# Cross-attention and mixture-of-experts in two layers: the second layer's keys made between the pieces of the first layer's shared expert

## The reference

```
x = x + tanh(g_xattn[0]) * cross_attention_0(layernorm(x), ctx)
x = x + tanh(g_ffn[0])   * (shared_expert(n) + routed_experts(n, top 1 of 8))   # n = layernorm(x)
x = x + tanh(g_xattn[1]) * cross_attention_1(layernorm(x), ctx)
x = x + tanh(g_ffn[1])   * mixture_1(layernorm(x), top 2 of 8)

def _swiglu(x, wg, wu, wd):
    return jax.nn.silu(x @ wg.T) * (x @ wu.T) @ wd.T
shared_out = _swiglu(x, shared_gate, shared_up, shared_down)      # layer 0, hidden width 512
k = (y @ Wk + bk).reshape(B, M, NUM_HEADS, HEAD_DIM)              # layer 1: y is ctx, not x
```

## Time and profile before

| | us |
|---|---|
| median of 3 runs | 1487.17 (1486.02 to 1487.17) |
| the profiled execution | 1488.32 |
| its span | 1486.5 |
| TensorE busy | 1352.8 (91% of the span) |
| ScalarE busy | 982.6 (66%) |
| VectorE busy | 539.6 (36%) |
| GpSimd busy | 175.0 (12%) |

### The profile page before, as it was taken

The page is one execution under the profiler, slowest core; times in us unless marked ns, Lnnn a source line. Parts: engine busy times, 40 slices in busy tenths (PEclk is TensorE's granted clock), DMA queues, the critical chain, the costliest instruction groups (busy, mean ns, idle before and its releaser), DMA issues. The chain is left out here.

```text
span 1486.5 us, 31922 instructions
## 1 busy us (share of the span) xinstructions
PE 1352.8 (91%) x13236; PEld 715.3 (48%) x13236; DVE 539.6 (36%) x1204; ACT 982.6 (66%) x1178; POOL 175.0 (12%) x188
## 2 busy tenths in 40 slices
PE   7799999999999996999869999999999985399994
PEld 4433333333333653899733334334334323299983
DVE  7412142241433253333461123322422433644435
ACT  4499999999997233222259995995995980155532
POOL 2000000000000330233300000000000000166530
PEclk9899999999999998999978999999999997599997
DMA  7671010101001814111338010110111215012223
GB/s 208 157 125 27 20 27 20 27 20 27 23 20 28 294 57 151 58 50 47 104 110 149 20 28 14 34 27 16 34 27 47 65 33 167 18 62 75 72 67 157
DMA packets 65867, 100.82 MB, mean 68 GB/s; under 512 B 10075, under 2 KB 47967, under 8 KB 64953
## 3 DMA queue, kind: packets, MB, share of 16 engines
q1 hardware_dynamic: 59768, 82.47, 20.5%
q0 software_dynamic: 5952, 16.26, 3.4%
HBM read 67.99 MB, written 26.21 MB: 63 GB/s over the span
## 5 line engine op out<-in xcount | busy, mean ns | idle before, releaser
L1232 ACT ACTIVATE arena<-ps 128x1024 f32<-128x1024 f32 x556 | 554.5, 1224 | 56.7 <-PE ps L998 56.7
L998 PE MATMUL ps<-arena 99*32 99x512 bf16 x6656 | 465.5, 384 | 16.8 <-PEq L848 10.9
L998 PEld LDWEIGHTS ps<-arena 99*32 99x32 bf16 x6656 | 149.8, 95 | 408.5 <-issue 168.2
L1232 ACT ACTIVATE wqkv<-ps 128x1024 f32<-128x1024 f32 x276 | 294.9, 1225 | 22.7 <-PE ps L998 22.7
L1014 PE MATMUL ps<-arena 128*32 128x512 f32 x2224 | 289.7, 593 | 1.3 <-ACT arena L1232 0.8
L1314 DVE COPY work<-ps 128x512 f32<-128x512 f32 x32 | 22.1, 691 | 406.6 <-PE ps L1014 406.6
L1704 PEld LDWEIGHTS ps<-work,arena 128*128 128x128 f32 x1184 | 145.1, 196 | 6.4 <-DVE work L1801 3.4
L1704 PE MATMUL ps<-work,arena 128*128 128x128 f32 x1184 | 146.2, 279 | 2.1 <-DVE work L1801 2.1
L1014 PE MATMUL ps<-wqkv,arena 128*32 128x512 f32 x1104 | 143.9, 593 | 0.0
L1905 POOL DMA_INDIRECT work<-xn_img,fetch x62 | 60.3, 973 | 613.4 <-POOLq L978 596.8
L1716 PE MATMUL ps<-arena,work 128*128 x496 | 117.2, 380 | 0.0
(11 more groups left out here) (206 smaller groups left out, 1158.7 us busy)
## 6 DMA issues: line engine op xcount, KB each, us to landing
arena<-in_ew SPq DMA_DIRECT2D x16, 512.0 KB, 5.6
arena<-q_img SPq DMA_DIRECT2D x32, 192.0 KB
arena<-y_tok SPq DMA_DIRECT2D x12, 512.0 KB, 6.3
arena<-k_img SPq DMA_DIRECT2D x8, 624.0 KB, 13.3
q_img<-work SPq DMA_DIRECT2D x18, 256.0 KB, 2.5
k_img<-work SPq DMA_DIRECT2D x21, 208.0 KB, 2.5
arena<-q_img SPq DMA_DIRECT2D x32, 128.0 KB
work<-work SPq DMA_DIRECT2D x128, 32.0 KB, 1.9
```

What stands on the lines that cost most here:

```text
L998: last = nc.tensor.matmul(ps[i * VW:(i + 1) * VW, buf + j, :], k2[0:ROWS + SHIFT, h, at:at + VW], q2[0:ROWS + SHIFT, h, :], start=True, st ...
L1232: nc.scalar.activation(probs[(b * STEPS + u) % RING], ps[:, buf:buf + 2, :], ACT.Exp, scale=SCALE).then_inc(s_exp, 1)
```

## The change

The core of the diff:

```diff
-                    def k_item(n):
-
-                        for ko in range(KD):
-                            if n:
-                                pe.wait_ge(s_kh, (n - 1) * KD + ko + 1)
-                            project_k(1, ko, n, (7, 5)[ko]).then_inc(s_kp, 1)
+                    def k_half(n, ko):
+                        if n == 0 and ko == 0:
+                            pe.wait_ge(s_tok, 1)
+                            pe.wait_ge(s_wk[1], 48)
+                        elif ko == 0:
+                            pe.wait_ge(s_kh, n * KD)
+                        else:
+                            pe.wait_ge(s_kh, n * KD + 1)
+                        project_k(1, ko, n, 5).then_inc(s_kp, 1)
...
                         shared_up(3, 0)
+                        k_half(0, 0)
                         shared_down(2)
-                        for f in range(1, 4):
-                            shared_up(3, f)
+                        k_half(0, 1)
                         lists()
+                        k_half(1, 0)
+                        shared_up(3, 1)
+                        k_half(1, 1)
+                        k_norm(0)
...
                         shared_down(3)
-                        pe.wait_ge(s_sy, NT)
-                        pe.wait_ge(s_wk[1], 48)
-                        k_item(0)
-                        for n in range(1, 4):
-                            k_item(n)
-                            k_norm(n - 1)
                         k_norm(3)
...
+                    def k_half(n, ko):
+                        act.wait_ge(s_kp, n * KD + ko + 1)
+                        if ko == 0:
+                            if n:
+                                act.wait_ge(s_kl, n)
+                            if n >= 2:
                                 act.wait_ge(s_kd[n % 2], 48)
+                        src = ps[:, 5, 0:KB]
+                        nc.scalar.activation(full1[:, ko, :], src, ACT.Copy)
...
+                        places()
+                        split_keys(0)
+                        shared_hidden(3, 0)
+                        shared_hidden(3, 1)
+                        for n in range(1, 3):
+                            split_keys(n)
+                            shared_hidden(3, n + 1)
+                        split_keys(3)
+                        for t in range(TB):
+                            n = TB * GP + t
+                            dve.wait_ge(s_sd, n + 1)
...
+                        for n in range(4):
+                            sp.wait_ge(s_kl, n + 1)
+                            store_parts(sp, k_img[1], part1[n % 2], slice(n * KB, (n + 1) * KB), False, s_kd[n % 2])
+                        sp.wait_ge(s_e, 16 * (2 * E + DOWN_KEPT))
                         sp.wait_ge(s_sd, NT)
                         sp.wait_ge(s_sx, TB * GP)
                         for e in range(DOWN_KEPT, E):
                             load_down(sp, e)
...
+                        sp.wait_ge(s_kd[0], 96)
...
-                        sp.wait_ge(s_e, 16 * 3 * E)
...
                     def down(i):
+                        if l == 0 and i == 0:
+                            pe.wait_ge(s_e, 16 * 3 * E)
```

More of the change, by code:

```diff
@@ L250, in build @@
         w_now[1][1], at = view(work, at, [KD, F])
-        at = 2 * KD * QB
+        _, at = view(work, 2 * 2 * NT * E, [layers[0].slots, 3 * (layers[0].tiles + 1)], BF16)
+        _, at = view(work, at, [layers[0].slots, P], BF16)
+        full1, at = view(work, at, [KD, KB])
         part1 = [[None] * 3, [None] * 3]
@@ L256, in build @@
                 part1[i][j], at = view(work, at, [KD, KB], BF16)
[L257 to L260, removed]
         TS = 2 * NT
@@ L947, in layer @@
                                                   for w in ("up", "act", "hidden", "down", "out", "added"))
-            s_kp, s_kf, s_kh, s_ks, s_kn = (only(l == 0, f"k1_{w}")
-                                            for w in ("projected", "full", "high", "squared", "summed"))
+            s_kp, s_kh, s_ks, s_kn = (only(l == 0, f"k1_{w}")
+                                            for w in ("projected", "high", "squared", "summed"))
+            s_pl = only(l == 0, "places_made")
             s_kr, s_km, s_kl = (only(l == 0, f"k1_{w}") for w in ("rest", "mid", "low"))
@@ L1262, in shared_out @@
                                                  scale=tgate[:, 2:3]).then_inc(s_sy, 1)
[L1264 to L1269, removed]
-                                act.wait_ge(s_kd[n % 2], 48)
[L1271 to L1276, removed]
+                    def k_half(n, ko):
[4 more added lines that the diff above has]
+                            if n >= 2:
+                                act.wait_ge(s_kd[n % 2], 48)
+                        src = ps[:, 5, 0:KB]
+                        nc.scalar.activation(full1[:, ko, :], src, ACT.Copy)
+                        if n >= 2 and ko == 0:
+                            act.wait_ge(s_kn, n - 1)
+                        nc.scalar.activation(squares1[n % 2][:, ko, :], src, ACT.Square).then_inc(s_ks, 1)
+                        nc.scalar.activation(part1[n % 2][0][:, ko, :], src, ACT.Copy).then_inc(s_kh, 1)
                     if l == 1:
@@ L1296, in _ @@
                             shared_act(2, f)
+                        shared_act(3, 0)
+                        k_half(0, 0)
                         shared_out(2)
[L1298 to L1301, removed]
+                        k_half(0, 1)
+                        k_half(1, 0)
+                        shared_act(3, 1)
+                        k_half(1, 1)
+                        k_half(2, 0)
+                        shared_act(3, 2)
+                        k_half(2, 1)
+                        k_half(3, 0)
+                        shared_act(3, 3)
+                        k_half(3, 1)
                 @block.vector
@@ L1495, in places @@
                                                              in1=pad[:, 0:NTL], op0=ALU.add, op1=ALU.add))
-                        nc.vector.tensor_scalar(fetch[:, 0:NTL], dest[:, 0:NTL], S - 1, None, ALU.bitwise_and)
+                        last = nc.vector.tensor_scalar(fetch[:, 0:NTL], dest[:, 0:NTL], S - 1, None, ALU.bitwise_and)
+                        if l == 0:
+                            last.then_inc(s_pl, 1)
                     def shared_hidden(b, f):
@@ L1509, in _ @@
                     else:
[L1510 to L1518, removed]
@@ L1519, in _, with split_keys @@
-                        places()
-                        for n in range(4):
+                        def split_keys(n):
                             dve.wait_ge(s_kh, KD * (n + 1))
-                            nc.vector.tensor_tensor(rest1, full1[n % 2], part1[n % 2][0], ALU.subtract
-                                                    ).then_inc(s_kr, 1)
+                            nc.vector.tensor_tensor(full1, full1, part1[n % 2][0], ALU.subtract).then_inc(s_kr, 1)
                             dve.wait_ge(s_kr, n + 1)
-                            nc.vector.tensor_copy(part1[n % 2][1], rest1).then_inc(s_km, 1)
+                            nc.vector.tensor_copy(part1[n % 2][1], full1).then_inc(s_km, 1)
```

22 lines of the change are left out of this document (16 added, 6 removed).

## The result

The changed kernel takes 1483.66 us (median of 12 runs, 1481.10 to 1486.93), the kernel before 1486.51 in the same comparison (12 runs, 1484.90 to 1491.21): a ratio of 0.9982 with an interval of 0.9974 to 0.9991. The forecast was 1482.7, with a range of 1480.4 to 1486.7.

A forecast was written before the change was run, and what follows sets the result against it. SyncE's last issue was taken to bound the routed experts' start: 2.2 us from TensorE's earlier norm plus 2.3 from SyncE's shorter tail give 4.5, from median 1487.17 to 1482.7 us; range 1480.4 to 1486.7.

The forecast's parts named there:

- a landing of the first fetch over 6 us: Sign of being wrong: GpSimd's first fetch for the routed experts takes over 6 us from issue, against 4.9 forecast.
- The wait for `s_tok`: Before the first key half, TensorE would idle 1.96 us until VectorE's L1467 line ends, starting at 540.63.
- The second rival: One fall of TensorE's clock in the wait at 540, costing 2.9 us: 1485.6 us; chance 0.08.
- The hand-over: In the keys, a half waiting for ScalarE to empty the same PSUM bank starts 3.10 us after the previous half.
- The fourth rival: Single-bank hand-overs take some 0.7 us longer in four places, or places and first split delay ScalarE: 1485.5 us; chance 0.07.
- The single `full1`: ScalarE could take `k_half(1,0)` only when this buffer was free, at 554.95; that wait stays hidden, 0.7 us to spare.
- The parts were late because 4 x 512 KB of down matrices were in flight: In the kernel before, down matrices issued at 564.66 explained ScalarE's 3.94 us wait for key parts to land.
- Rival three: TensorE's clock falls repeatedly between 540 and 583 us, 2.9 us each; three falls give 1491.4 us; chance 0.05.
- The wait ahead of the third tile of the last `shared_down`: On TensorE, a new wait of 1.1 us for VectorE's addition of the first tile to x, until 579.32.
- TensorE's last norm 2.2 us earlier, SyncE's tail 2.3 us shorter: At the block's end, TensorE's norm ends at 583.3, not 585.53; SyncE's last issue follows by 1.8, not 4.08 us.
- The fetch's landing: GpSimd's first fetch, ahead of the routed experts, was taken to land 4.9 us after issue, unchanged.
- The first rival: The fetch waits for down matrices issued right ahead of it, costing up to 3.0 us: 1485.7 us; chance 0.11.

The follow-up runs named there:

- SyncE's part alone: Kernel before, with only SyncE's new order: key stores before the four down-matrix loads, their landing awaited by TensorE; keys not interleaved; 1489.63 us, ratio 1.0018 to before.
- fetch first: Changed kernel, with the last four down matrices and next layer's weights loaded only after the first fetch has landed; 1479.64 us, ratio 0.9952 to before.
- all together: Changed kernel plus more PSUM banks, `shared_down(2)` ahead of the first key halves, and loads after the first fetch's landing; 1472.82 us, ratio 0.9894 to before.
- the changed kernel's second comparison: The changed kernel measured again without any edit, against another set of runs of the kernel before; 1485.35 us, ratio 0.9986.

## Why the prediction was right, point by point

It was right in direction and range, with less gain than forecast: 2.85 us in the total and 3.43 in the stretch, where 4.5 stood. In the total, a part of the agreement is luck: the median of before is 0.66 us lower in this comparison than the 1487.17 from which the forecast was counted. Of its own signs of being wrong, one came: a landing of the first fetch over 6 us. By its own steps:

- *The wait for `s_tok`, 1.96 us*: 1.81. Right, and the clock was 1.00 in every 5 us from 535 to 580. The second rival is refuted.
- *The hand-over, 3.10 from half to half in one bank*: 550.09 - 547.10 = 2.99. The 0.1 is on the first step: ScalarE reads 1.60 us after TensorE begins instead of 1.70. *The period, 7.98*: 7.93. The fourth rival is refuted.
- *The single `full1`, hidden with 0.7 us to spare*: ScalarE takes `k_half(1,0)` at 552.91, when the first split is over, and ends its third pass at 554.25, 0.78 before `k_half(1,1)`.
- *"The parts were late because 4 x 512 KB of down matrices were in flight"*: this reading of the kernel before was for the most part wrong. With the matrices gone from there ("SyncE's part alone"), ScalarE still waits 3.48 of its 3.94 us. No term of the sum hangs on it, since the interleaving removes the wait either way.
- *Rival three, repeated falls of the clock*: 1.00 in both stretches from 549 to 583. The five waits, 0.79 to 1.81 us, left it alone in every kernel that was run with them. The Trainium skill (TensorE: Matmul & The Clock Gate, "A second HAM failure mode: psum-queue depth-cycling") tells of short idles between groups of matmuls that make the clock fall and return; no run here shows that, with eight halves through one bank. The one longer wait, 2.64 us, was followed by the pieces at half speed (5.91 instead of 3.04 us, in SyncE's part alone), once and not again and again.
- *The wait ahead of the third tile of the last `shared_down`, 1.1 us*: the second pair of tiles starts 577.14 - 572.65 = 4.49 after the first, 1.03 more than the 3.46 of two tiles.
- *TensorE's last norm 2.2 us earlier, SyncE's tail 2.3 us shorter*: the norm ends 51.46 us into the stretch instead of 53.83, so 2.37; the tail is 582.95 - 581.21 = 1.74 instead of 4.08, so 2.34. Sum 4.71, where 4.5 was forecast.
- *The fetch 1.35 behind the last issue*: 1.35.
- **The fetch's landing, "I take 4.9 as before, since the bandwidth was taken then too"**: this term was mis-sized. It took 6.18 and 6.21. The bandwidth was not taken in the same measure: before, the fetch ran beside the weights alone (4.9 to 5.4); now four loads of 512 KB had been issued in the 3.4 us ahead of it. The first rival had the mechanism right, as far as the queues show it. The fetch's first packet begins 4.8 us after issue, when the matrices are nearly through, and the fetch lands 0.91 us behind the last of them (590.44 and 589.53); without the weights it is 0.36, and without either the first packet begins at 1.84 us and the landing takes 2.94. What the rival had wrong is the price, up to 3.0 where 1.28 was lost. The matrices by themselves were to be through 0.5 us behind the forecast landing (591.9 and 591.4), and the rest was for weights behind them; in the run the matrices were through 0.33 us later than a landing of 4.90, and 0.95 more passed until TensorE began. So the forecast's number held although its first rival's mechanism came, because the mechanism cost less than the rival had for it; "4.9 as before" was not sound. The Trainium skill (DMA: Bandwidth & Descriptors, "Queues, rings and completion order") says that a DMA engine takes turns between the queues for which it has work. The trace shows both queues at work together only once the fetch's packets have begun; what holds them back until then is not shown, and stays open.
- *No wait at the first down product*: none, 601.98 - 590.48 = 11.50 as before (11.51), and no expert's matrices are waited for.

The stretch therefore gained 3.43 us where 4.5 was forecast: 4.71 up to the fetch, 0.2 more than forecast, less the 1.28 of the landing. The total gained 2.85 us in one comparison and 1.4 in the other. From the first down product to the end, where the change touches nothing, it is 879.1 us before, 877.3 in the changed kernel's profile and 879.9 in its second one: these two differ by more than the disputed microsecond. In the kernels that gain, the median total gains 0.5 to 1.1 us less than the stretch (fetch first: 8.2 in the stretch, 7.1 in the total; all together: 15.0 and 14.3), and 2.0 less in the changed kernel's second comparison (3.4 and 1.4). A part of it can lie between the first turned rows and the first down product, 11.51 us before and 11.5 to 12.2 in the others; since "all together" has only 10.98 there and loses 0.7 all the same, that isn't the whole of it, and where the rest goes stays open.

## What to carry to other kernels

When the last instruction of a block is moved earlier, ask what was moved next to the transfer that everybody waits for: here the four loads that left the middle of the block ran ahead of the gather that starts the next one, and took back 1.3 of 4.7 us. The remedy that worked is order: start the small transfer on which an engine waits, let it land, and only then issue the large ones that have time. And before single waits are filled with more work, look whether they are there because two pieces share a PSUM bank: a second bank was worth 1.24 us in each of two places.

## What the runs showed of the hardware

- An indirect fetch of GpSimd's into on-chip memory, from its issue to TensorE's start on its rows, took 2.94 to 2.96 us with no load of SyncE's beside it, 4.90 to 5.41 beside the next weights (two loads of 512 KB and two of 128 KB), 5.60 beside 2 MB of down matrices issued up to 3.4 us earlier, and 6.17 to 6.49 beside both. Its first packet begins 1.84 us after issue in the quiet, 3.0 to 3.2 beside the weights, and behind the matrices 4.2 to 4.9, when their 2.10 MB are all but moved. It is the small transfer that waits: with the fetch behind them, the last matrix lands 7.1 us after its issue in four executions (7.6 in "SyncE's part alone"), and 7.1 with no fetch beside them.
- Waits of 0.79 to 1.81 us between groups of matmuls, five within 40 us, cost their own length and nothing more: the clock stayed at 2.4 GHz. Those of 2.64, 3.10 and 3.26 us, each behind a light norm, were followed by work at 1.2 GHz. Length alone doesn't decide it: behind the pause ahead of the last stage's products, 2.65 to 3.10 us, the clock was at 1.2 GHz in eight executions, but at 2.4 GHz from the start in "SyncE's part alone" (2.96) and "all together" (2.91).
- Where the clock returns there varies from run to run: the same 64 matmuls took 16.96 to 17.10 us in seven executions, 15.52 in the changed kernel's first, and 14.05 in the two at 2.4 GHz throughout. That alone moves a total by up to 3 us, whatever the kernel: "SyncE's part alone", which is slower than before, is one of the two.
